# A group's maximum over TensorE and VectorE, ScalarE tables loaded ahead, the residual in x's own buffer, on one core of a Trainium2

## What is computed

```
x = x + conv_part(ln_over_channels(x))      # attention to 16 centers, per quarter image and head
t = tokens of x                             # one row of 96 channels per pixel
t = t + ffn(ln(t))                          # 96 -> 384 -> 96 with sign weights

def ffn(x):
    h = quantize(x @ sign(W1) + b1)
    h = gelu(h)
    return quantize(h @ sign(W2) + b2)

def quantize(x):                            # 5 groups along the batch, n // 5 = 6 images each
    for g in range(5):
        gamma = max(abs(x[group g]))        # one number over 6 images
        out[group g] = clip(x[group g] * 128 / (gamma + 1e-5), -128 + 1e-5, 128 - 1e-5)
    # images 30 and 31 stay zero here, so for them the FFN adds nothing
```

## Time and profile before

| | |
|---|---|
| median of three runs | 3116.61 us (3114.12 to 3118.87) |
| the profiled execution, its own time | 3116.98 us |
| its span in the trace | 3115.2 us |
| busy: PE / DVE / ACT / POOL | 94% / 87% / 73% / 61% |
| instructions | 63469 |
| mean granted clock of TensorE | 0.97 |
| HBM traffic over the span | 48 GB/s |

### The profile page before, as it was taken

The page is one execution under the profiler, slowest core; times in us unless marked ns, Lnnn a source line. Parts: engine busy times, 40 slices in busy tenths (PEclk is TensorE's granted clock), DMA queues, the critical chain, the costliest instruction groups (busy, mean ns, idle before and its releaser), DMA issues.

```text
span 3115.2 us, 63469 instructions
## 1 busy us (share of the span) xinstructions
PE 2921.4 (94%) x20760; PEld 2028.8 (65%) x20760; DVE 2713.4 (87%) x5896; ACT 2259.5 (73%) x4628; POOL 1888.7 (61%) x4668
## 2 busy tenths in 40 slices
PE   3999999989999998999999989999998999999885
PEld 2677776557777755777776567777755767775553
DVE  3788888989999988999998989999988999998976
ACT  1677777977777778777777967777787777777843
POOL 1677766347777733777775357777734777774253
PEclk9999999999999999999999999999989999998987
DMA  2011111012222100222221012222200222210024
GB/s 49 17 33 32 32 41 39 1 38 72 64 63 63 56 24 16 64 63 63 63 64 48 1 47 63 63 71 63 63 9 24 65 69 71 71 55 24 17 78 124
DMA packets 30939, 154.79 MB, mean 50 GB/s; under 512 B 6483, under 2 KB 6676, under 8 KB 30612
## 3 DMA queue, kind: packets, MB, share of 16 engines
q1 hardware_dynamic: 30612, 150.74, 17.4%
HBM read 76.06 MB, written 74.66 MB: 48 GB/s over the span
## 4 chain that ended last, share of the span: by engine, by line
POOL 44%; PE 31%; issue 20%; DVE 2%; ACT 2%; POOLq 0%; SPq 0%; DMA 0%; DVEq 0%; ACTq 0%
PE ps L1017 9%; PE ps L1055 8%; POOL eq L438 5%; POOL mo_x L387 5%; POOL mo_t L387 5%; PE ps L942 4%; POOL nxy L416 3%; POOL ninv L421 3%; POOL ny L414 3%; POOL mo_x L380 3%; POOL nxy L418 2%; POOL cinv L428 2%; PE ps L906 2%; POOL mo_t L372 1%; POOL n2c L402 1%
## 5 line engine op out<-in xcount | busy, mean ns | idle before, releaser
L942 PE MATMUL ps<-wfT,xn 97*112 97x384 f32 x1792 | 724.9, 512 | 10.3 <-ACT sq L517 3.8
L1017 PE MATMUL ps<-tok,w1T 98*128 98x392 f16 x2880 | 613.3, 337 | 25.1 <-ACT turns L576 23.1
L517 ACT ACTIVATE sq<-ps 112x384 f32<-112x384 f32 x896 | 431.9, 490 | 199.1 <-PE ps L942 195.6
L769 DVE TENSOR_REDUCE hmax<-ps 128x1 f32<-128x392 f32 x720 | 393.3, 560 | 60.3 <-PE ps L1017 48.2
L1017 PEld LDWEIGHTS ps<-tok,w1T 98*128 98x128 f16 x2880 | 285.2, 99 | 229.7 <-issue 49.9
L942 PEld LDWEIGHTS ps<-wfT,xn 97*112 97x112 f32 x1792 | 272.5, 180 | 197.9 <-issue 48.7
L689 DVE TENSOR_REDUCE n<-sq 112x32 f32<-112x1536 f32 (+1 forms) x256 | 393.8, 1538 | 3.0 <-ACT sq L517 0.2
L453 POOL CAST turns<-turns 128x392 f16<-128x392 f32 x240 | 169.6, 707 | 338.3 <-ACT turns L573 334.3
L573 ACT ACTIVATE turns<-ps,scale 128x1176 f32<-128x1176 f32 x240 | 367.8, 1532 | 7.7 <-PE ps L1017 4.5
L478 ACT ACTIVATE xnT<-ps,mo_x 112x96 f32<-112x96 f32 x896 | 304.4, 449 | 67.5 <-POOL mo_x L389 67.4
L840 DVE SCALAR_TENSOR_TENSOR turns<-turns 128x1176 f16<-128x1176 f32 x240 | 333.2, 1388 | 0.0
(11 more groups left out here) (130 smaller groups left out, 6363.7 us busy)
## 6 DMA issues: line engine op xcount, KB each, us to landing
xbuf<-in_x SPq DMA_DIRECT2D x64, 588.0 KB, 4.7
out<-xbuf SPq DMA_DIRECT2D x64, 588.0 KB, 3.7
turns<-out SPq DMA_DIRECT2D x60, 588.0 KB, 6.4
out<-turns SPq DMA_DIRECT2D x60, 588.0 KB, 3.7
cst<-in_constants SPq DMA_DIRECT2D x1, 644.0 KB
tok<-in_L_ffn_W SPq DMA_DIRECT2D x2, 142.5 KB
wf<-in_L_conv_Wf SPq DMA_DIRECT2D x1, 144.0 KB
tok<-in_L_conv_Wv SPq DMA_DIRECT2D x1, 144.0 KB
```

The costliest lines, as they stand in the source:

```text
L517: nc.scalar.activation(sq[:, t, :], bank(2 + t % 2, TN, D), ACT.Square).then_inc(f_sq, 1)
L769: v.tensor_reduce(o, bank(6 + u % 2, 128, HT), AX.X, ALU.max, apply_absolute_value=True)\
L942: mm(bank(2 + t % 2, TN, D), xn[:, k % 2, t * TN:(t + 1) * TN], wfT[:, :], start=True, stop=True)\
L1017: ins = mm(dst, w1T[:, c * 128:(c + 1) * 128], tok[:, bass.ds(place, 1), part, s * HT:(s + 1) * HT].rearrange("p a n -> p (a n)"), start=p ...
```

## The change

It has four parts.

1. The maximum over partitions moves from GpSimd to TensorE and VectorE. `column_to_row` multiplies the column with the identity into a row of 128 in PSUM, `largest_of_row` reduces it, `row_to_column` multiplies the number with a row of ones so that it stands on all partitions, and `group_scale` reads it from PSUM. For y, `group_scale` now stands at the end of the group and not in the next one.
2. ScalarE runs an activation of one column, whose result nobody reads, before a stage needs another table: GELU before the wait for the scale, Sigmoid ahead of the third last `y_out` of a group.
3. `residual` writes into `xbuf` where it reads x. `tq` and `place_t` go. The store of t waits for the residual, the next load of x for the transposes.
4. An FFN unit is 14 full rows of a half image and no longer a 28 by 28 quarter. Its first unit needs the residual of both quarters, so X, M, A, R become 4, 3, 2, 0. `finish` works on dense rows.

```diff
-        tq = sb("tq", [C, 2, QN])
...
+        ahead = sb("ahead", [128, 1])
...
-        g_max, g_all, g_eps, g_rec, g_scale = (sem(n) for n in ("g_max", "g_all", "g_eps", "g_rec", "g_scale"))
+        g_max, g_T, g_row, g_all, g_eps, g_rec, g_scale = (sem(n) for n in ("g_max", "g_T", "g_row", "g_all", "g_eps", "g_rec", "g_scale"))
...
-        X, M, A, R = 3, 2, 1, 0
+        X, M, A, R = 4, 3, 2, 0
...
-                    done(sp, "t_placed", g * GQ + b * BODY + (2 * j + 1))
+                    done(sp, "t_done", g * GQ + b * BODY + (2 * j + 1))
...
+                    done(sp, "t_T", g * GQ + b * BODY + (2 * j + 1))
...
-                    done(sp, "t_placed", GROUPS * GQ + (2 * (h // 3) + 1))
+                    done(sp, "t_done", GROUPS * GQ + (2 * (h // 3) + 1))
...
-            def over_partitions(n, i):
-                pool.wait_ge(g_max, n)
-                nc.gpsimd.partition_all_reduce(gam[:, i, 1:2], gam[:, i, 0:1], 128, MAX).then_inc(g_all, 1)
...
-                over_partitions(2 * g + 1, 0)
...
-                over_partitions(2 * g + 2, 1)
...
-            def place_t(k, q, place, use):
-                done(act, "t_done", q)
-                nc.scalar.copy(image_rows(k), tq[:, k % 2, :].rearrange("c (r w) -> c r w", w=QS))\
-                    .then_inc(S["t_placed"], 1)
...
-                        (X, 1, normalise("x", 0, 1)), (R, 1, place_t), (X, 1, copy_x(0)), (X, 1, copy_x(1)),
+                        (X, 1, normalise("x", 0, 1)), (X, 1, copy_x(0)), (X, 1, copy_x(1)),
...
+                    if isinstance(place, int) and place == GQ - 2 and k % 2 == 1:
+                        nc.scalar.activation(ahead[:, :], ones[:, 0:1], ACT.Sigmoid)
...
+                nc.scalar.activation(ahead[:, :], ones[:, 0:1], ACT.Gelu)
...
-            def residual(half, part):
+            def residual(half):
...
-                    if half == 0:
-                        done(dve, "t_placed", q - 2)
-                        if part != "last":
-                            done(dve, "t_T", q - 2)
...
-                    t = tq[:, k % 2, lo:hi].rearrange("c (r w) -> c r w", w=QS)
-                    ins = v.scalar_tensor_tensor(t, o, bpc[:, :], image_rows(k, lo // QS, (hi - lo) // QS), ALU.add, ALU.add)
+                    t = image_rows(k, lo // QS, (hi - lo) // QS)
+                    ins = v.scalar_tensor_tensor(t, o, bpc[:, :], t, ALU.add, ALU.add)
...
+            def largest_of_row(n, i):
+                dve.wait_ge(g_T, n)
+                v.tensor_reduce(gam[0:1, i, 1:2], bank(7, 1, 128), AX.X, ALU.max).then_inc(g_row, 1)
...
-                v.tensor_scalar(den[:, i, 0:1], gam[:, i, 1:2], EPS_Q, None, ALU.add).then_inc(g_eps, 1)
+                v.tensor_scalar(den[:, i, 0:1], bank(7, 128, 1, 128), EPS_Q, None, ALU.add).then_inc(g_eps, 1)
...
-                        group_scale(2 * g, 1)
...
-                    t = fin[:, k // 2 % 2, :].rearrange("c (r w) -> c r w", w=SIDE)[:, :, k % 2 * QS:(k % 2 + 1) * QS]
-                    v.scalar_tensor_tensor(t, y_of(place).rearrange("c (r w) -> c r w", w=QS), -QCLIP, t,
-                                           ALU.max, ALU.add).then_inc(S["final"], 1)
+                    t = fin[:, k // 2 % 2, k % 2 * QN:(k % 2 + 1) * QN]
+                    v.scalar_tensor_tensor(t, y_of(place), -QCLIP, t, ALU.max, ALU.add).then_inc(S["final"], 1)
...
-                         (X, 1, pooled), (M, 1, cosine), (X, 1, centers), (A, 1, residual(0, part)),
-                         (R, 1, h_largest(5, 6), FFN), (A, 1, residual(1, part)), (X, 1, center_floor),
+                         (X, 1, pooled), (M, 1, cosine), (X, 1, centers), (A, 1, residual(0)),
+                         (R, 1, h_largest(5, 6), FFN), (A, 1, residual(1)), (X, 1, center_floor),
...
+                largest_of_row(2 * g + 1, 0)
...
+                largest_of_row(2 * g + 2, 1)
+                group_scale(2 * g + 2, 1)
...
-            def to_tokens(s, b0):
+            def to_tokens(s, b0, g=0):
...
-                        done(pe, "t_done", q)
+                        done(pe, "t_done", q + 1 - k % 2)
...
+                        if isinstance(place, int) and place == 0 and not (isinstance(g, int) and g == 0):
+                            pe.wait_ge(g_eps, 2 * g)
...
-                        src = (xq if s == "x" else tq)[:, k % 2, t * TN:(t + 1) * TN]
+                        if s == "x":
+                            src = xq[:, k % 2, t * TN:(t + 1) * TN]
+                        else:
+                            src = xbuf[:, k // 2, k % 2 * QN + t * TN:k % 2 * QN + (t + 1) * TN]
...
-            def attention():
+            def attention(g):
...
-                        (M, 0, features(1, 2)), (R, 0, to_tokens("t", 6), FFN), (M, 0, features(2, 4)),
+                        (M, 0, features(1, 2)), (R, 0, to_tokens("t", 6, g), FFN), (M, 0, features(2, 4)),
...
+            def column_to_row(n, i):
+                pe.wait_ge(g_max, n)
+                tr(bank(7, 1, 128), gam[:, i, 0:1], ident).then_inc(g_T, 1)
+            def row_to_column(n, i):
+                pe.wait_ge(g_row, n)
+                mm(bank(7, 128, 1, 128), ones[0:1, 0:128], gam[0:1, i, 1:2], start=True, stop=True).then_inc(g_all, 1)
...
-                pipeline(pe, g, part, attention())
+                pipeline(pe, g, part, attention(g))
...
+                    if place == 0 and k == 0:
+                        row_to_column(2 * g + 1, 0)
...
+                column_to_row(2 * g + 1, 0)
...
+                column_to_row(2 * g + 2, 1)
+                row_to_column(2 * g + 2, 1)
...
-            pipeline(pe, GROUPS, "last", attention())
+            pipeline(pe, GROUPS, "last", attention(GROUPS))
```

More of the change, by code:

```diff
@@ L72, in build @@
     ALU, ACT, AX = mybir.AluOpType, mybir.ActivationFunctionType, mybir.AxisListType
-    MAX = bass.bass_isa.ReduceOp.max
     ctx = ExitStack()
@@ L180, in build @@
             n_square1 n_part1 n_factor1 n_newton2 n_square2 n_part2 n_factor2 n_newton3 cos_done sig_done top_done eq_done
-            eqT_ps eqT_copied first_ps sim_done simT_ps0 simT_ps simT_copied0 simT_copied u_ps u_done a_ps a_rden a_mul a_half a_done o_ps0 o_ps t_done t_placed
+            eqT_ps eqT_copied first_ps sim_done simT_ps0 simT_ps simT_copied0 simT_copied u_ps u_done a_ps a_rden a_mul a_half a_done o_ps0 o_ps t_done
             t_T t_stats t_sum t_dif t_m2 t_half t_d2 t_v t_var t_rstd t_shift t_norm0 t_norm n_ps0 n_ps n_hi0 n_hi n_lo0 n_lo c_min final""".split()
```

## The result

| | before | after |
|---|---|---|
| median, runs taken side by side | 3115.36 us (3112.48 to 3118.87) | 3084.61 us (3082.44 to 3084.96) |
| the profiled execution, its own time | 3116.98 us | 3084.92 us |
| its span | 3115.2 us | 3083.0 us |

The ratio is 0.9904, with a 95% interval of 0.9893 to 0.9916: about 30 us faster. The forecast was 3085.

The account below looks back on a forecast made before the run. TensorE, with VectorE close behind, was taken to bound the middle slots, leaving the ten maxima and the program's start and end. 3116.98 - 17 - 21 + 17 - 11 = 3085 us; own range 3073 to 3099, with both clock cases and dear lead 3060 to 3103.

Parts of the forecast that it names:

- First maximum, -17: Maximum of h, five times: column to GELU falls from 5.45 or 6.75 us to 3.3; 17 us gained in all.
- An earlier GELU shifts the whole second pass: After the first maximum: ScalarE sets the pace of the second pass, so time gained before GELU is gained throughout.
- Second maximum, -21: Maximum of y, five group ends: 20 us from earlier transposes plus 1 us from the clock; 21 us gained.
- So its transposes start at 658.2 + 1.8 - 0.6 = 659.4: Group end: TensorE's transposes of `eq` start at 659.4 instead of 663.49; 4.1 us each, 20 us in five.
- So I count only 1 us of 11: Stretch from those transposes to the next step: a high clock would gain 2.2 us per group; only 1 us counted.
- The added slot, +17: Start of the program: one more complete attention slot without FFN costs 17 us, bounds 15 and 21.
- The end, -11: End of the program: the last units drain a slot sooner, giving back 11 us, bounds 8 and 13.
- The slots, 0: Middle slots stay at 18.7 to 18.8 us; the prediction is wrong if they move by more than 0.1 us.
- Copy of t, whole rows, 0: ScalarE's copy of t, 110 us in all, goes while ScalarE waits for TensorE; `final` handles as many elements: 0.
- The clock stays high: Rival: TensorE's clock stays high through the boundaries of both maxima, 15 us more gain, 3070 us; chance 13%.
- ScalarE's freed time: Rival: it shortens about 125 slots by 0.1 to 0.2 us each, 12 to 25 us, 3060 to 3073; chance 8%.
- The dear version: Rival: added slot costs 21, end gives back only 8, maxima chains 0.2 us more per hop; 3102 us, chance 13%.

Follow-up runs that it names:

- e6: Changed kernel with unread matmuls filling idle TensorE at the second maximum (9 before the wait for y, 2 between the small products): 3070.32 us, 0.9865 of the kernel before.
- e8: Changed kernel with the second maximum's two small products moved behind the next slot's first two feature steps: 3070.82 us, 0.9868 of the kernel before.
- e7: Changed kernel with 12 unread matmuls filling TensorE ahead of the first maximum: 3094.56 us, 0.9945 of the kernel before.
- e5: Changed kernel with a GpSimd reduction put back at each group's end, its result unread and nobody waiting: 3102.02 us, 0.9964 of the kernel before.
- e10: Changed kernel with both the unused GpSimd reduction and the filling matmuls at the second maximum: 3104.11 us, 0.9966 of the kernel before.
- e3: Kernel before with only the residual written over x, no copy of t, whole rows and one slot more: 3123.34 us, 1.0022 of the kernel before.
- e1: Kernel before with only the two group maxima moved to TensorE and VectorE: 3098.17 us, 0.9937 of the kernel before.
- e12: e9 with unread filling matmuls in the last part as well, 15 per slot: 3062.58 us, 0.9840 of the kernel before.
- e2: Kernel before with only ScalarE's tables loaded ahead by two tiny activations: 3112.09 us, 0.9974 of the kernel before.
- e4: Changed kernel without the residual part (3 slots, copy of t kept): 3097.88 us, 0.9929 of the kernel before.
- e9: e4 with filling matmuls at the second maximum: 3068.63 us, 0.9855 of the kernel before.
- e11: Changed kernel with filling matmuls at both the first and the second maximum: 3076.98 us, 0.9883 of the kernel before.

## Why the prediction was right

The time was right to the microsecond, and that is in part luck. The mechanism was right: GpSimd's reduction and its return held both maxima, and the added slot is nearly paid back at the end. But two terms of the sum were wrong inside, a gain at the fifth boundary was lost again behind it, and 2.6 us that I had not counted made up for most of that.

**First maximum, -17: right as a sum.** 3.3 us of chain became 3.6, at the low clock as assumed; the small products are listed with 0.37 and 0.58 us and not 0.29, the matmuls between them with 2.17 and not 2.05. The chain brought 14.7, where my working gave 16 and I took 17 without a row for the one more. The pass behind it brought 2.2, which I had not forecast and cannot explain; together 16.9. "An earlier GELU shifts the whole second pass" held only in part: in the filled kernels e6 and e8 column of h to column of y was 109.3 us in every group, whether GELU came after 3.0 or 3.6. I take it that TensorE and not ScalarE sets the pace there; no run tests it. With TensorE filled ahead of this maximum (e7) the chain was 2.34 us, the 2.3 of the prediction's high clock.

**Second maximum, -21: right as a sum (22.0), wrong in both parts.** The failed step is "So its transposes start at 658.2 + 1.8 - 0.6 = 659.4". That is 6.2 us after the column. It was 5.9 in two groups, 8.1 in one and 10.2 to 10.3 in two: 11.2 us gained where the step has 20. It took the features at the high pace, as the earlier trace rows show them before, though TensorE's new idle ahead of them, which the next paragraph of the prediction speaks of, can cost that pace. The other step is "So I count only 1 us of 11": the stretch behind the transposes was 3.95 us in all five groups and brought 10.8. TensorE had then been busy since the small products, and its clock was back. The low pace used to lie behind the transposes, with up to 6.7 us for work of 3.95; it now lies ahead of them, with 8.2 us for work of 4.6, and in some groups only. e6 and e8 show that it is this idle: without it all five stay high. That the two errors, 9 us too much and 10 too little, cancel is luck. e5 and e10 show that the rest of the step, GpSimd's return, was right.

**The added slot, +17: right**, 17.7, less 1.4 that the start before it was shorter; the time up to the first slot differs by up to 3 us between runs of like kernels (87.4 to 90.7 in these traces).

**The end, -11: right where it stands alone.** From the last column of y it was 162.2 us and is 151.2; e3 has 150.4. But 4 us of these 11 are in the fifth boundary, which I had already counted above. e1 shows it: its fifth boundary is 3.9 us shorter, and from the last column of y to the end it took 162.0 against 162.2. The last part took back what the boundary gave; the slots there follow the clock in part (e12). So the terms were -17, -18, +16 and -11, and -2.6 in the slots.

**The slots, 0: nearly.** 18.73 us where it was 18.76. That is not put down to the change: e3, which has the third part, had 18.77 like e1, e2 and e4, which have not; e5 to e8, with it, had 18.73; and e9 without it and e11 with it, run together, both had 18.75. What sets it stays open. In the 2.6 us is also a loss: the first full slot of a group grew from 18.32 to 18.65 us.

**Copy of t, whole rows, 0: right.** e3 contains them and costs no more than its slot. ScalarE's wait for `xn` grew from 74.7 us:

```profile
ACT xn L495 <- PE ps L905: 151.5, 254, 1.1
```

**The rivals.** "The clock stays high" came true in two boundaries and a part of a third, of ten. e6, at 3070, has the rival's time but not its sum: 11 us from the second boundaries and 5 behind the last of them, with the first maxima still at the low clock. ScalarE's freed time shortened nothing. The residual in place slowed nothing, and GpSimd makes no exchange any more. The dear version did not come.

## What to carry to other kernels

A rare instruction of an engine can cost most by what it delays on that engine: leave it in with nobody waiting for it (e5), and its own price shows. When a wait at a boundary goes, ask next what TensorE's clock does there; a few matmuls without use ahead of the boundary are a cheap test, here worth over a third of what the change brought. Parts of a change that meet at such a place don't add up (-20, -8 and +7 made -30), so each is judged with the clock held.

## What the runs showed of the hardware

- With equal work and equal gaps (1.59 and 0.37 us) a boundary ran at 1.2 GHz in one group and at 2.4 GHz in the next of the same execution. With the first gap at 0.67 us (e8), or both filled (e6), all five were at 2.4.
- After a reduction over partitions of 0.36 or 0.38 us GpSimd needed 7.6 to 8.6 us until its next `tensor_tensor` started, whether or not anyone waited for the reduction (the kernel before, e2, e3, e5 and e10, five times each). A cast behind one started after 1.92 us, when its input came (group 0, before).
- Two casts of one pass, GpSimd's at 0.70 us and VectorE's at 0.37, can fall into a phase where they take 3.2 and 0.64, and 0.67 and 0.35, in turn (means 1.83 and 0.51) to the end of the pass; it cost 4 us of 105.
- A column's maximum over 128 partitions took 1.4 us by two small products and a row reduction at the high clock (1235.00 to 1236.36, up to the scale's first step), where GpSimd's reduction began 4.5 us after group 0's first column. Behind casts, at the second column, GpSimd's began after 0.10 us and took 0.36; there its price was the return.
